# First sublayer's projections as three products of high and low halves, on one core of a Trainium2 chip

## The chip, the cores and the metric

The kernel runs on one core of one Trainium2 chip. The metric is the device time of one execution in microseconds (us), as the median of several executions; lower is better. The engines are named as in the profile: PE (TensorE, matrix products; PEld is its weight load), DVE (VectorE), ACT (ScalarE), POOL (GpSimd), and SP, which here only issues DMAs. Each runs its own list of instructions in order and waits on semaphores that the others raise.

## The reference

Four rows of 1024 tokens with 128 features pass through four sublayers, each behind a layer norm and added to its input: a linear-attention block, a mixture of 32 experts, a windowed attention, and the same mixture again. The change touches the first sublayer. Cut to it:

```python
def _L0_attn_a_ref(x, Wq, Wk, Wv, lambda_params, g1, g2, g3, W1, W2):
    xn = _rms(x, g1)                                   # x is the layer norm of the input
    Q, K, V = xn @ Wq.T, xn @ Wk.T, xn @ Wv.T          # as 16 heads of 8
    pQ, pK = elu(Q), elu(K)
    Q1, Q2 = split(pQ); K1, K2 = split(pK)             # halves of a head
    kv1, kv2 = K1 (x) V * SCALE, K2 (x) V * SCALE      # summed over the heads of a token
    attn = Q1 kv1 - lmb * Q2 kv2
    attn = (1.0 - LAMBDA_INIT) * _rms(attn, g2)
    attn = _rms(attn, g3) + attn
    return gelu(attn @ W1) @ W2 + attn
x = x + _L0_attn_a_ref(_layernorm(x), ...)
x = x + _L0_ffn_ref(_layernorm(x), gate_w, gate_up_w, down_w)      # 32 experts, 8 per token
x = x + _L0_attn_b_ref(_layernorm(x), w_qkv, w_out, b_out)         # window of 64
x = x + _L0_ffn_ref(_layernorm(x), gate_w, gate_up_w, down_w)
```

## The kernel before, in words

A row of 1024 tokens is two groups of 512 (T = 4 tiles of 128 tokens). The mixture of experts is the bulk of the work: each pass of a group through it is a stage of 16 chunks (two experts each). In a chunk PE forms gate and up with six products of 512 columns (high and low halves of inputs and weights, lines 1489 to 1491), ACT applies silu (L1030), DVE multiplies by up (L1270), POOL multiplies by the token's weight for the expert (L847), and three chunks later PE multiplies by `down_w` in plain fp32 (L1512, two instructions per product). Everything else is fitted between chunks as named steps. A table written by hand (`PLAN`, `SPECIAL`) says behind which chunk of which stage each step is done; `AHEAD` does the same for the start, before the first stage. Every engine walks the same table and does its own part of each step, so a step's place in the table is its place in the order of every engine that has a part in it.

The steps of the first sublayer for a group are `x_stats` (DVE), `x_rstd` (POOL), `x_apply` (ACT, writes the normed tiles `z`), `x_turn` (PE transposes `z` into the PSUM bank `side`, ACT copies it to `zT`), then four times `qkv` (PE multiplies a tile of `zT` by `qkv_a_w`, 384 columns; ACT copies it to `qkv` and starts `elu`), `attend` (POOL, `kv_terms`), `kvsum`, `wterm`, `wred` (DVE), the norms per head and token `h_sq1` to `h_gain`, and `h_sum` (DVE), which writes `attn_sum`; `x_add` (POOL) and `attnT` (PE) read that. The projections come under three names: `qkv_first` for the first group of row 0, `qkv_next` for the first group of row 1, `qkv` for the others.

All steps that use the bank `side` take turns. Before PE writes it, it waits until the semaphore `side_taken` has counted every earlier use as taken (`side_free`). A use is taken when its reader has finished; for `x_turn` that is ACT's copy into `zT`:

```python
def copy_side(dst, row, name, n):
    side_product(row, name, n)
    act.activation(dst, side, ACT.Copy).then_inc(side_taken, 1)
```

`x_turn` runs eight times (ACT line 897, output `zT`): at 10, 28, 58, 122, 267, 343, 501 and 572 us of the span. The first three stand in `AHEAD`. In it, DVE's order before the change at the second one is `elu_first` 3, then `kvsum` 1, since `x_turn` has no part on DVE.

Of the kernel before, what the change touches and what calls it, by code (L numbers as in the profile page):

```python
# [80 lines left out]
def back(*steps):  # L81
# [246 lines left out]
AHEAD = own(  # L328
    ("masks", 0), ("x_stats", 0), ("x_rstd", 0), ("x_apply", 0), ("x_stats", 1), ("w_hi", 0), ("masks", 1), ("x_rstd", 1),
    ("x_turn", 0), ("qkv_first", 0), ("qkv_first", 1), ("lam", 0), ("elu_first", 0), ("attend", 0), ("qkv_first", 2),  # L330
    ("elu_first", 1), ("qkv_first", 3), ("kvsum", 0), ("elu_first", 2), ("attend", 1), ("wterm", 0), ("wred", 0),
# [89 lines left out]
def hybrid_block(nc, x, wqkv_a, lam, g1, g2, g3, w1, w2, wqkv_b, wout, bout, wgate, wg, wu, wd, out):  # L421
# [3 lines left out]
    with ExitStack() as ctx:  # L425
        def sb(name, shape, dt=F32):
            return ctx.enter_context(nc.sbuf_tensor(name, shape, dt))

        def sem(name):
            return ctx.enter_context(nc.semaphore(name))  # L430


        qkv_a_w = sb("qkv_a_w", [P, 3 * D])
        w1_w, w2_w = sb("w1_w", [P, D]), sb("w2_w", [P, D])
# [24 lines left out]

        zT = sb("zT", [P, GT])  # L460
        qkv = sb("qkv", [P, T, 3 * D])
        elu = sb("elu", [P, T, 2 * D])
        kv_terms, w_terms = sb("kv_terms", [P, 2, HD * HD * H]), sb("w_terms", [P, H * HD * HD])
        kv = sb("kv", [P, HD * HD])
        attn, squares = sb("attn", [P, G, T, D]), sb("squares", [P, T, D])
        head_ms, head_rms = sb("head_ms", [P, T * H]), sb("head_rms", [P, T * H])
        newton = sb("newton", [P, T * H])
        tok_ms, tok_rms = sb("tok_ms", [P, T]), sb("tok_rms", [P, T])
        gain = sb("gain", [P, T, D])
        attn_sum = sb("attn_sum", [P, T, D])  # L470
        attnT = sb("attnT", [P, GT])
# [21 lines left out]
        mixT = sb("mixT", [P, TILES, P])  # L493
        mix_all = sb("mix_all", [P, NB * P])

        bank = [ctx.enter_context(nc.psum_tensor(f"bank{i}", [P, 512], F32))[:] for i in range(8)]
# [5 lines left out]
        gate_loaded, up_loaded = sem("gate_loaded"), sem("up_loaded")  # L502
        pool_const, ident_ready, masks_ready = sem("pool_const"), sem("ident_ready"), sem("masks_ready")
        lam_step, qkv_w_ready, bits_ready, head_mask_ready = (
            sem("lam_step"), sem("qkv_w_ready"), sem("bits_ready"), sem("head_mask_ready"))
# [37 lines left out]

        qkv_a_loads = [(qkv_a_w[:], wqkv_a), (g1_col[:], g1.rearrange("(p a) -> p a", a=1))]
        attn_a_loads = [(lam_row[:], lam.partition_broadcast(P)), (g2_row[:], g2.partition_broadcast(P)),
# [3 lines left out]
        def wait(engine, semaphore, count):  # L549

            if count > 0:
                engine.wait_ge(semaphore, count)
# [4 lines left out]
        def group(row, g):  # L557
            return row * G + g
# [164 lines left out]
        def _(pool):  # L723
# [105 lines left out]
            def x_add(row, g):  # L829
                pool.wait_ge(attn_ready, group(row, g) + 1)  # L830
                x = x_of(row)[:, T * g:T * g + T]
                pool.tensor_tensor(x, x, attn_sum[:], ALU.add).then_inc(attn_added, 1)

# [53 lines left out]
        def _(act):  # L887
# [22 lines left out]
            def x_turn(row, g):  # L910
                copy_side(zT[:], row, "x_turn", g)

# [178 lines left out]
        def _(dve):  # L1091
# [7 lines left out]
            def norm_stats(row, kind, n):  # L1099
# [104 lines left out]
            def h_sum(row, g):  # L1204
                dve.wait_ge(gain_ready, group(row, g) + 1)
                wait(dve, attn_a_done, group(row, g))
                dve.tensor_tensor(attn_sum[:], attn[:, g], gain[:], ALU.mult).then_inc(attn_ready, 1)

# [57 lines left out]
            def gated(row, f, s):  # L1266
# [6 lines left out]
            steps = {"x_stats": lambda row, n: norm_stats(row, "x", n), "m_stats": lambda row, n: norm_stats(row, "m", n),  # L1273
                     "s_stats": lambda row, n: norm_stats(row, "s", n), "lam": lam_step_coef, "elu": elu_step, "elu_first": elu_of_first, "w_hi": w_hi, "w_lo": w_lo, "kvsum": kvsum, "wterm": wterm, "wred": wred,
                     "h_red1": h_red1, "h_newton1": h_newton1, "h_newton2": h_newton2, "h_scale": h_scale, "h_red2": h_red2, "h_sum": h_sum, "mlp2": mlp2,
# [3 lines left out]
            dve.wait_ge(qkv_a_loaded, 16 * len(qkv_a_loads))  # L1279
            dve.tensor_scalar(qkv_a_w[:], qkv_a_w[:], g1_col[:, 0:1], None, ALU.mult).then_inc(qkv_w_ready, 1)  # L1280
            dve.wait_ge(attn_a_loaded, 16 * len(attn_a_loads))
# [3 lines left out]
            step(dve.tensor_scalar(g2_row[:], g2_row[:], 1.0 - LAMBDA_INIT, None, ALU.mult))  # L1285
            run_ahead(steps, 2)

# [70 lines left out]
        def _(pe):  # L1358
# [3 lines left out]
            def turn(row, kind, n, name):  # L1362
# [4 lines left out]
                mm.then_inc(side_ready, 1)  # L1367

            def qkv_step(row, i):
                side_free(row, "qkv", i)  # L1370
                t = i % T
                pe.matmul(side[:, 0:3 * D], zT[:, P * t:P * (t + 1)], qkv_a_w[:],  # L1372
                          start=True, stop=True).then_inc(side_ready, 1)

            def qkv_first(row, i):
                if i == 0:
                    pe.wait_ge(qkv_w_ready, 1)
                    pe.wait_ge(side_taken, SIDE_AT[0, "x_turn", 0] + 1)
                pe.matmul(bank[i][:, 0:3 * D], zT[:, P * i:P * (i + 1)], qkv_a_w[:],
                          start=True, stop=True).then_inc(qkv_first_ready, 1)  # L1380

            def qkv_next(row, i):
                if i == 0:
                    pe.wait_ge(side_taken, SIDE_AT[row, "x_turn", 0] + 1)
                if i > 1:
                    pe.wait_ge(next_taken, i - 1)
                pe.matmul(bank[NEXT_BANKS[i % 2]][:, 0:3 * D], zT[:, P * i:P * (i + 1)], qkv_a_w[:],
                          start=True, stop=True).then_inc(next_ready, 1)

            def attnT_step(row, g):  # L1390
                pe.wait_ge(attn_ready, group(row, g) + 1)
                side_free(row, "attnT", g)
                for t in range(T):
                    mm = pe.transpose(side[:, P * t:P * (t + 1)], attn_sum[:, t], ident[:])
                mm.then_inc(side_ready, 1)
# [251 lines left out]
```

## Time and profile before

| | |
|---|---|
| median of 3 runs | 1011.01 us (1008.63 to 1011.54) |
| profiled execution, its own time | 1018.66 us |
| its span | 1016.9 us |
| busy: PE, DVE, ACT, POOL | 917.2, 643.8, 612.5, 660.4 us |
| granted PE clock, mean | 0.956 of 2.4 GHz |

The span runs from the first to the last instruction of the profiled execution; its own time is 1.8 us more. PE is busy for 90% of the span. Its first 100 us are different from the rest: there PE has little to do, and the other engines hand one group's work to each other.

### The profile page before, as it was taken

What the parts mean: (1) busy time and instruction counts of PE and PEld (TensorE: products, weight loads), DVE (VectorE), ACT (ScalarE), POOL (GpSimd) and SP (SyncE); (2) the same over time, 40 slices, a digit from 0 to 9 for tenths busy, and PEclk for the clock granted to TensorE, in tenths of its full rate; (3) what the DMA queues carried; (4) which work ended last, traced back from release to release, by engine and by line L of the source; (5) the groups of instructions that cost most, each with busy time, mean ns of one, the idle gap of its engine ahead of it and who ended that gap; (6) DMA issues with size and microseconds to landing.
All of it is one profiled execution on the core that took longest, in us unless ns stands there. A gap on an engine that the chain in (4) does not pass through costs nothing.

```text
span 1016.9 us, 16679 instructions
## 1 busy us (share of the span) xinstructions
PE 917.2 (90%) x5472; PEld 629.8 (62%) x5472; DVE 643.8 (63%) x1447; ACT 612.5 (60%) x1876; POOL 660.4 (65%) x610
## 2 busy tenths in 40 slices
PE   2366999899999999899999899999999998998998
PEld 1144656676666666587666556677666566666665
DVE  4877865687759647688739636778744247447432
ACT  4444756984664576876674566698465458376432
POOL 6676967566778749556759746756665446545654
PEclk8558999999999999979999999999999999999999
DMA  5004361114453544510433544530344661260362
GB/s 181 0 1 97 82 127 44 43 44 101 92 125 85 128 92 90 132 38 17 94 85 86 124 90 89 124 83 17 70 100 86 125 142 39 63 147 13 83 127 62
DMA packets 63320, 85.67 MB, mean 84 GB/s; under 512 B 3777, under 2 KB 29186, under 8 KB 62978
## 3 DMA queue, kind: packets, MB, share of 16 engines
q1 hardware_dynamic: 63234, 84.61, 36.8%
q8 instruction: 43, 0.70, 0.3%
q14 instruction: 43, 0.35, 0.1%
HBM read 79.32 MB, written 5.28 MB: 83 GB/s over the span
## 4 chain that ended last, share of the span: by engine, by line
PE 58%; ACT 14%; POOL 8%; DVE 7%; issue 5%; DMA 1%; DVEq 0%; SPq 0%; ACTq 0%; POOLq 0%
PE bank L1512 16%; PE bank L1489 8%; PE bank L1491 8%; PE bank L1490 8%; ACT probs L1055 6%; PE bank L1533 3%; POOL work L847 3%; PE bank L1548 3%; PE bank L1562 2%; POOL kv_terms L812 2%; ACT work L1030 1%; PE bank L1526 1%; POOL probs L855 1%; PE bank L1372 1%; PE bank L1366 1%
## 5 line engine op out<-in xcount | busy, mean ns | idle before, releaser
L847 POOL TENSOR_TENSOR work<-work,spread_w 128x512 f32<-128x512 f32 x256 | 338.3, 1333 | 179.8 <-DVE work L1270 155.6
L1270 DVE TENSOR_TENSOR work<-work,bank 128x512 f32<-128x512 f32 x256 | 174.4, 682 | 227.9 <-ACT work L1030 143.3
L1512 PE MATMUL bank<-work,down_w 128*128 128x512 f32 x512 | 266.1, 604 | 14.2 <-POOL work L847 9.1
L1030 ACT ACTIVATE work<-bank 128x512 f32<-128x512 f32 x256 | 150.9, 595 | 182.3 <-PE bank L1491 179.3
L1055 ACT ACTIVATE probs<-bank,neg_max 128x96 f32<-128x96 f32 x512 | 166.0, 383 | 12.3 <-DVE neg_max L1298 6.5
L1489 PE MATMUL bank<-z_hi,gate_hi 128*128 128x512 f32 x256 | 169.0, 660 | 2.5 <-ACT work L1030 1.8
L855 POOL TENSOR_TENSOR probs<-probs,prob_inv 128x768 f32<-128x768 f32 x64 | 94.1, 1470 | 73.0 <-DVE prob_inv L1306 73.0
L1055 ACT ACTIVATION_READ_ACCUMULATOR probs<-bank,neg_max 128x1 f32 x512 | 126.8, 250 | 0.0
L1512 PEld LDWEIGHTS bank<-work,down_w 128*128 128x128 f32 x512 | 95.6, 191 | 44.4 <-POOL work L847 14.5
L1491 PE MATMUL bank<-z_hi,gate_lo 128*128 128x512 f32 x256 | 102.1, 399 | 0.0
L1491 PE MATMUL bank<-z_hi,up_lo 128*128 128x512 f32 x256 | 101.8, 398 | 0.0
L1489 PE MATMUL bank<-z_hi,up_hi 128*128 128x512 f32 x256 | 101.8, 398 | 0.0
L1490 PE MATMUL bank<-z_lo,gate_hi 128*128 128x512 f32 x256 | 101.6, 397 | 0.0
L1490 PE MATMUL bank<-z_lo,up_hi 128*128 128x512 f32 x256 | 100.9, 394 | 0.0
L812 POOL TENSOR_TENSOR kv_terms<-elu,qkv 128x1024 f32<-128x1024 f32 x32 | 81.6, 2553 | 17.9 <-DVE elu L1127 14.8
L1312 DVE COPY probsT<-bank 96x512 f32<-96x512 f32 x128 | 80.3, 666 | 5.0 <-PE bank L1548 4.7
L1298 DVE TENSOR_REDUCE neg_max<-bank 128x4 f32<-128x384 f32 x128 | 64.9, 548 | 24.7 <-PE bank L1533 23.7
L1548 PE MATMUL bank<-ident,probs 128*96 128x128 f32 x512 | 71.4, 282 | 10.2 <-DVE probsT L1312 8.4
L1489 PEld LDWEIGHTS bank<-z_hi,gate_hi 128*128 128x128 f32 x256 | 49.1, 192 | 40.2 <-issue 30.5
L1533 PE MATMUL bank<-keysT,qm 32*128 32x96 f32 x1024 | 70.7, 273 | 0.0
L1490 PEld LDWEIGHTS bank<-z_lo,gate_hi 128*128 128x128 f32 x256 | 49.3, 193 | 34.1 <-issue 31.3
L1548 PEld LDWEIGHTS bank<-ident,probs 128*96 128x96 f32 x512 | 54.2, 128 | 23.0 <-issue 13.3
(154 smaller groups left out, 1481.0 us busy)
## 6 DMA issues: line engine op xcount, KB each, us to landing
spread_w<-comb_dram SPq DMA_DIRECT2D x126, 512.0 KB, 6.7
vals<-v_dram SPq DMA_DIRECT2D x16, 384.0 KB, 4.0
x_buf<-x SPq DMA_DIRECT2D x8, 256.0 KB, 3.2
v_dram<-v_tok SPq DMA_DIRECT2D x8, 256.0 KB, 5.0
out<-xs SPq DMA_DIRECT2D x8, 256.0 KB, 4.2
spread_w<-wg SPq DMA_DIRECT2D x1, 1024.0 KB, 7.2
spread_w<-wu SPq DMA_DIRECT2D x1, 1024.0 KB, 9.3
comb_dram<-combT SPq DMA_DIRECT2D x16, 64.0 KB, 1.6
```

Of the source, the lines that this page charges most:

```text
L812: pool.tensor_tensor(kv_terms[:, i % 2].rearrange("p (e d h) -> p e d h", e=HD, d=HD), k.unsqueeze(2).broadcast_to([P, HD, HD, H]), v.unsq ...
L847: pool.tensor_tensor(work[:, n % WORK], work[:, n % WORK], spread_w[:, n // EACH % 2, s % EACH], ALU.mult).then_inc(hid_gated, 1)
L855: pool.tensor_tensor(pr, pr, prob_inv[:, i % 2, part].unsqueeze(2).broadcast_to([P, HALF_BLOCKS, KW]), ALU.mult).then_inc(probs_normed, 1)
L1030: act.activation(work[:, n % WORK], bank[GATE_BANKS[ring_of(row, f, s)]], ACT.Silu).then_inc(silu_ready, 1)
L1055: a = act.activation(probs[:, i % 2, m], bank[hg][:, b * KW:(b + 1) * KW], ACT.Exp, bias=neg_max[:, i % 2, m:m + 1], accum_out=prob_sum[:, ...
L1270: dve.tensor_tensor(work[:, n % WORK], work[:, n % WORK], bank[UP_BANKS[ring_of(row, f, s)]], ALU.mult).then_inc(gated_ready, 1)
L1489: pe.matmul(dst, w_hi[:, cols], h, start=True, stop=False)
L1490: pe.matmul(dst, w_hi[:, cols], l, start=False, stop=False)
L1491: pe.matmul(dst, w_lo[:, cols], h, start=False, stop=True).then_inc(ready, 1)
L1512: pe.matmul(bank[Y_BANK], down_w[:, c], work[:, n % WORK], start=(c == 0), stop=(c == CH - 1)).then_inc(down_done, 1)
L1533: mm = pe.matmul(bank[hg][:, KW * b:KW * (b + 1)], qm[feats, i // T, NB * (i % T) + b].rearrange("p j q -> p (j q)"), keysT[feats, first:f ...
L1548: mm = pe.transpose(bank[4 + b % 2][0:KW, P * hg:P * (hg + 1)], probs[:, i % 2, hg * NB + b], ident[:])
```

## The change

The weights `qkv_a_w` and the turned inputs `zT` are each split into a high half (a copy rounded to F32R) and a low half (what the copy left out). Each projection is then three products instead of one fp32 product. The low half of the input is formed by DVE out of the bank `side`, so `x_turn` gets a part on DVE, `x_lo`; the bank is taken when that has run. The weights are split by DVE in two more instructions at the start. `x_turn` 0 is moved ahead in `AHEAD`. `squares` and `gain` share one buffer, the raw weights are loaded into `mix_all`, and `h_sum` writes its product over `attn`, so `attn_sum` and a wait go.

```diff
 AHEAD = own(
-    ("masks", 0), ("x_stats", 0), ("x_rstd", 0), ("x_apply", 0), ("x_stats", 1), ("w_hi", 0), ("masks", 1), ("x_rstd", 1),
-    ("x_turn", 0), ("qkv_first", 0), ("qkv_first", 1), ("lam", 0), ("elu_first", 0), ("attend", 0), ("qkv_first", 2),
+    ("masks", 0), ("x_stats", 0), ("x_rstd", 0), ("x_apply", 0), ("x_turn", 0), ("x_stats", 1), ("w_hi", 0),
+    ("masks", 1), ("x_rstd", 1), ("qkv_first", 0), ("qkv_first", 1), ("lam", 0), ("elu_first", 0), ("attend", 0), ("qkv_first", 2),
...
-        attn, squares = sb("attn", [P, G, T, D]), sb("squares", [P, T, D])
+        attn, scratch = sb("attn", [P, G, T, D]), sb("scratch", [P, T, D])
+        squares = gain = scratch
...
+        qkv_a_w = mix_all[:, 0:3 * D]
...
             def x_turn(row, g):
-                copy_side(zT[:], row, "x_turn", g)
+                side_product(row, "x_turn", g)
+                act.activation(zT_hi[:], side, ACT.Copy).then_inc(x_hi_ready, 1)
...
+            def x_lo(row, g):
+                dve.wait_ge(x_hi_ready, group(row, g) + 1)
+                dve.tensor_tensor(zT_lo[:], side, zT_hi[:], ALU.subtract).then_inc(side_taken, 1)
...
             def h_sum(row, g):
                 dve.wait_ge(gain_ready, group(row, g) + 1)
-                wait(dve, attn_a_done, group(row, g))
-                dve.tensor_tensor(attn_sum[:], attn[:, g], gain[:], ALU.mult).then_inc(attn_ready, 1)
+                dve.tensor_tensor(attn[:, g], attn[:, g], gain[:], ALU.mult).then_inc(attn_ready, 1)
...
-            dve.tensor_scalar(qkv_a_w[:], qkv_a_w[:], g1_col[:, 0:1], None, ALU.mult).then_inc(qkv_w_ready, 1)
+            step(dve.tensor_scalar(qkv_a_w, qkv_a_w, g1_col[:, 0:1], None, ALU.mult))
+            step(dve.tensor_copy(qkv_a_hi[:], qkv_a_w))
+            dve.tensor_tensor(qkv_a_lo[:], qkv_a_w, qkv_a_hi[:], ALU.subtract).then_inc(qkv_w_ready, 1)
+            x_lo(0, 0)
...
+            def project(dst, t, ready):
+                h, l = zT_hi[:, P * t:P * (t + 1)], zT_lo[:, P * t:P * (t + 1)]
+                pe.matmul(dst, h, qkv_a_hi[:], start=True, stop=False)
+                pe.matmul(dst, h, qkv_a_lo[:], start=False, stop=False)
+                pe.matmul(dst, l, qkv_a_hi[:], start=False, stop=True).then_inc(ready, 1)
+
             def qkv_step(row, i):
                 side_free(row, "qkv", i)
-                t = i % T
-                pe.matmul(side[:, 0:3 * D], zT[:, P * t:P * (t + 1)], qkv_a_w[:],
-                          start=True, stop=True).then_inc(side_ready, 1)
+                project(side[:, 0:3 * D], i % T, side_ready)
```

`qkv_first` and `qkv_next` call `project` in the same way, and `x_add` and `attnT` read `attn[:, g]`.

The order of DVE's instructions changes where `x_lo` enters. At the second `x_turn` of the start, where the sums of the first group's tiles follow each other (`elu` is `elu_first`, `kv` is `kvsum`, `w_terms` is `wterm`, `attn` is `wred`), DVE had before:

```order
16 L1162 TENSOR_TENSOR w_terms<-elu,kv 128x1024
17 L1168 TENSOR_REDUCE attn<-w_terms 128x128
18 L1132 SCALAR_TENSOR_TENSOR elu<-elu,qkv 128x256
19 L1138 TENSOR_REDUCE kv<-kv_terms 128x8x8
20 L1162 TENSOR_TENSOR w_terms<-elu,kv 128x1024
21 L1168 TENSOR_REDUCE attn<-w_terms 128x128
```

and has now, from the same tile on:

```order
19 L1168 TENSOR_TENSOR w_terms<-elu,kv 128x1024
20 L1174 TENSOR_REDUCE attn<-w_terms 128x128
21 L1138 SCALAR_TENSOR_TENSOR elu<-elu,qkv 128x256
22 L1123 TENSOR_TENSOR zT_lo<-bank,zT_hi 128x512
23 L1144 TENSOR_REDUCE kv<-kv_terms 128x8x8
24 L1168 TENSOR_TENSOR w_terms<-elu,kv 128x1024
25 L1174 TENSOR_REDUCE attn<-w_terms 128x128
```

The subtraction stands between the last `elu_first` and `kvsum` 1, and with it DVE's wait for the turned and copied tiles of the second group.

At the `x_turn` of row 3's first group (501 us before), in the slot behind chunk 9 of a stage, DVE had before the choice of experts (`MAX`, `neg_top`, `MATCH_REPLACE`), `h_sum`, and the next chunks' products (`work`):

```order
507 L1241 MAX top<-logits 128x8 x4
508 L1243 TENSOR_SCALAR neg_top<-top 128x4
509 L1245 MATCH_REPLACE replaced<-top,logits 128x32 x4
510 L1207 TENSOR_TENSOR attn_sum<-attn,gain 128x512
511 L1270 TENSOR_TENSOR work<-work,bank 128x512 x2
```

and has now:

```order
515 L1246 MAX top<-logits 128x8 x4
516 L1248 TENSOR_SCALAR neg_top<-top 128x4
517 L1250 MATCH_REPLACE replaced<-top,logits 128x32 x4
518 L1212 TENSOR_TENSOR attn<-attn,scratch 128x512
519 L1123 TENSOR_TENSOR zT_lo<-bank,zT_hi 128x512
520 L1275 TENSOR_TENSOR work<-work,bank 128x512 x2
```

The subtraction, which frees the bank for the first projection of that group behind chunk 10, comes last of the slot's steps.

## Rows read from the trace of the kernel before

**Rows 1.** The page, chain that ended last, shares of the span by engine.

```profile
PE 58%; ACT 14%; POOL 8%; DVE 7%; issue 5%; DMA 1%; DVEq 0%; SPq 0%; ACTq 0%; POOLq 0%
```

**Rows 2.** The chain in order of time, 264 to 270 us: start, us, what.

```profile
267.73 0.23 PE bank L1491
267.96 0.86 PE bank L1512 x2
268.82 0.65 PE bank L1372 x2
```

**Rows 3.** A group of DVE by line and shape: busy us, mean ns, idle before.

```profile
L1225 DVE TENSOR_TENSOR z_lo<-bank,z_hi 128x512 fp32r<-128x512 f32 x16 | 11.0, 685 | 5.1 <-ACT z_hi L981 5.1
```

**Rows 4.** Timeline of the first projections: start, us, engine, line, [idle before, releaser].

```profile
10.59 0.16 DVE L1282 TENSOR_TENSOR lam_prod<-lam_row 128x2 f32<-128x2 f32 x1 [5.30 <-DMA router_w<-wgate]
10.76 5.29 PE L1379 MATMUL bank<-qkv_a_w,zT 128*128 128x384 f32 x8 [0.78 <-ACT zT L897]
...
12.42 0.49 ACT L922 ACTIVATE qkv<-bank 128x384 f32<-128x384 f32 x1 [1.80 <-PE bank L1379]
...
13.70 0.49 ACT L922 ACTIVATE qkv<-bank 128x384 f32<-128x384 f32 x1
```

**Rows 5.** Timeline of DVE, 23 to 37 us.

```profile
23.26 1.30 DVE L1132 SCALAR_TENSOR_TENSOR elu<-elu,qkv 128x256 f32<-128x256 f32 x1
24.48 1.21 DVE L1138 TENSOR_REDUCE kv<-kv_terms 128x64 f32<-128x1024 f32 x1
...
34.48 1.22 DVE L1168 TENSOR_REDUCE attn<-w_terms 128x128 f32<-128x1024 f32 x1
36.48 0.69 DVE L1173 TENSOR_REDUCE head_ms<-squares 128x64 f32<-128x512 f32 x1 [0.77 <-ACT squares L959]
```

**Rows 6.** Timeline of ACT at the second turn.

```profile
24.99 1.63 ACT L906 ACTIVATE z<-x_buf,shift,rstd 128x128 f32<-128x128 f32 x4
27.83 0.60 ACT L897 ACTIVATE zT<-bank 128x512 f32<-128x512 f32 x1 [1.20 <-PE bank L1366]
```

**Rows 7.** Timelines of DVE, PE and ACT at the third turn.

```profile
57.95 1.19 DVE L1138 TENSOR_REDUCE kv<-kv_terms 128x64 f32<-128x1024 f32 x1
...
58.76 2.93 PE L1387 MATMUL bank<-qkv_a_w,zT 128*128 128x384 f32 x4 [0.69 <-ACT zT L897]
...
61.78 0.49 ACT L939 ACTIVATE qkv<-bank 128x384 f32<-128x384 f32 x1 [0.57 <-PE bank L1387]
...
62.44 1.64 ACT L906 ACTIVATE z<-x_buf,shift,rstd 128x128 f32<-128x128 f32 x4
```

**Rows 8.** Timelines of DVE and POOL, on to the first weighted chunk.

```profile
65.91 0.69 DVE L1225 TENSOR_TENSOR z_lo<-bank,z_hi 128x512 fp32r<-128x512 f32 x1 [4.21 <-ACT z_hi L981]
...
88.05 1.27 POOL L847 TENSOR_TENSOR work<-work,spread_w 128x512 f32<-128x512 f32 x1
```

**Rows 9.** Timeline of DVE, end of the choice of experts at 268 us.

```profile
268.61 0.17 DVE L1245 MATCH_REPLACE8 replaced<-top,logits 128x32 f32<-128x32 f32 x1
```

**Rows 10.** The chain and DVE's timeline at row 3's first turn.

```profile
502.92 0.65 PE bank L1372 x2
...
503.43 0.69 DVE L1207 TENSOR_TENSOR attn_sum<-attn,gain 128x512 f32<-128x512 f32 x1
```

**Rows 11.** Timelines of ACT, DVE and PE behind row 3's second turn.

```profile
571.53 0.60 ACT L897 ACTIVATE zT<-bank 128x512 f32<-128x512 f32 x1 [1.23 <-PE bank L1366]
...
571.51 1.28 DVE L1187 TENSOR_SCALAR newton<-head_ms 128x64 int32<-128x64 int32 x1
...
573.83 0.88 DVE L1113 BATCH_NORM_STATS2 stats<-xs 128x6 f32<-128x128 f32 x4
...
580.93 0.63 PE L1366 MATMUL bank<-ident,z 128*128 128x128 f32 x4 [2.26 <-DVEq L1216]
```

**Rows 12.** A long wait of PE, and the stretch behind it (PEclk is the granted clock).

```profile
806.48 1.13 PE L1446 MATMUL bank<-seqT,qkv_b_w 128*128 128x512 f32 x2 [2.02 <-DVEq L1216]
...
808.00:810.00 2.00, 2.00 (x6) 1.52 (x6) 0.00 (x0) 2.00 (x5) 0.00 (x0) 0.50 0.00 0
```

More of the change, by code:

```diff
@@ L430, in sem @@
             return ctx.enter_context(nc.semaphore(name))
-        qkv_a_w = sb("qkv_a_w", [P, 3 * D])
+        qkv_a_hi, qkv_a_lo = sb("qkv_a_hi", [P, 3 * D], F32R), sb("qkv_a_lo", [P, 3 * D], F32R)
         w1_w, w2_w = sb("w1_w", [P, D]), sb("w2_w", [P, D])
@@ L458, in hybrid_block @@
         z = sb("z", [P, NORM_RING, T, D])
-        zT = sb("zT", [P, GT])
+        zT_hi, zT_lo = sb("zT_hi", [P, GT], F32R), sb("zT_lo", [P, GT], F32R)
         qkv = sb("qkv", [P, T, 3 * D])
@@ L468, in hybrid_block @@
         tok_ms, tok_rms = sb("tok_ms", [P, T]), sb("tok_rms", [P, T])
-        gain = sb("gain", [P, T, D])
-        attn_sum = sb("attn_sum", [P, T, D])
         attnT = sb("attnT", [P, GT])
@@ L503, in hybrid_block @@
         pool_const, ident_ready, masks_ready = sem("pool_const"), sem("ident_ready"), sem("masks_ready")
+        x_hi_ready = sem("x_hi_ready")
         lam_step, qkv_w_ready, bits_ready, head_mask_ready = (
@@ L542, in hybrid_block @@
         head_added = sem("head_added")
-        qkv_a_loads = [(qkv_a_w[:], wqkv_a), (g1_col[:], g1.rearrange("(p a) -> p a", a=1))]
+        qkv_a_loads = [(qkv_a_w, wqkv_a), (g1_col[:], g1.rearrange("(p a) -> p a", a=1))]
         attn_a_loads = [(lam_row[:], lam.partition_broadcast(P)), (g2_row[:], g2.partition_broadcast(P)),
@@ L831, in x_add @@
                 x = x_of(row)[:, T * g:T * g + T]
-                pool.tensor_tensor(x, x, attn_sum[:], ALU.add).then_inc(attn_added, 1)
+                pool.tensor_tensor(x, x, attn[:, g], ALU.add).then_inc(attn_added, 1)
             steps = {"w_lo": w_lo, "masks": masks, "attend": attend, "h_rg": h_rg, "h_pow2": h_pow2, "x_add": x_add,
@@ L1273, in _ @@
             steps = {"x_stats": lambda row, n: norm_stats(row, "x", n), "m_stats": lambda row, n: norm_stats(row, "m", n),
-                     "s_stats": lambda row, n: norm_stats(row, "s", n), "lam": lam_step_coef, "elu": elu_step, "elu_first": elu_of_first, "w_hi": w_hi, "w_lo": w_lo, "kvsum": kvsum, "wterm": wterm, "wred": wred,
+                     "s_stats": lambda row, n: norm_stats(row, "s", n), "x_turn": x_lo, "lam": lam_step_coef, "elu": elu_step, "elu_first": elu_of_first, "w_hi": w_hi, "w_lo": w_lo, "kvsum": kvsum, "wterm": wterm, "wred": wred,
                      "h_red1": h_red1, "h_newton1": h_newton1, "h_newton2": h_newton2, "h_scale": h_scale, "h_red2": h_red2, "h_sum": h_sum, "mlp2": mlp2,
@@ L1285, in _ @@
             step(dve.tensor_scalar(g2_row[:], g2_row[:], 1.0 - LAMBDA_INIT, None, ALU.mult))
-            run_ahead(steps, 2)
+            run_ahead(steps, 5)
             dve.wait_ge(bits_ready, 1)
@@ L1378, in qkv_first @@
                     pe.wait_ge(side_taken, SIDE_AT[0, "x_turn", 0] + 1)
-                pe.matmul(bank[i][:, 0:3 * D], zT[:, P * i:P * (i + 1)], qkv_a_w[:],
-                          start=True, stop=True).then_inc(qkv_first_ready, 1)
+                project(bank[i][:, 0:3 * D], i, qkv_first_ready)
             def qkv_next(row, i):
@@ L1386, in qkv_next @@
                     pe.wait_ge(next_taken, i - 1)
-                pe.matmul(bank[NEXT_BANKS[i % 2]][:, 0:3 * D], zT[:, P * i:P * (i + 1)], qkv_a_w[:],
-                          start=True, stop=True).then_inc(next_ready, 1)
+                project(bank[NEXT_BANKS[i % 2]][:, 0:3 * D], i, next_ready)
             def attnT_step(row, g):
@@ L1393, in attnT_step @@
                 for t in range(T):
-                    mm = pe.transpose(side[:, P * t:P * (t + 1)], attn_sum[:, t], ident[:])
+                    mm = pe.transpose(side[:, P * t:P * (t + 1)], attn[:, g, t], ident[:])
                 mm.then_inc(side_ready, 1)
```

## The prediction

> **What bounds the kernel now.** I read the page first, for the chain that ended last: more than half of it is PE [rows 1]. That share is a mean over two different stretches, so I then read the chain in order of time. From about 100 us on PE's products stand in it back to back over long stretches: a product of high and low halves takes a place of 0.23 us at 512 columns, an fp32 product of 512 columns 0.86, and a projection of 384 columns 0.65 [rows 2]. There, what a step costs PE is what it costs the kernel, and 17 of the 20 projections that fall behind 100 us are pieces of that chain. Before 100 us PE hardly counts. I read the timelines of the other engines there and looked for the one whose instructions leave no gap. It is DVE: from the `elu` at 23.26 to the `wred` that starts at 34.48 each instruction starts as the one before it ends, and ACT's squares and the norms follow on that last sum [rows 5]. The chain goes on with `z_lo` at 65.91 and ends at POOL's first weighted chunk at 88.05 [rows 8]; in between, each engine waits for the one before it, and nothing there is tied to a fixed time such as a load from outside.
>
> **Splitting the weights** adds two DVE instructions of 384 columns in a stretch where DVE sits idle for 5.30 us [rows 4]. A subtraction of 512 columns takes 0.685 us [rows 3], so both together stay under 1.4 us. They cost nothing; without that cover they would cost about that.
>
> **The first turn.** The bank was free for PE when ACT's copy ended, and PE began at 10.76 [rows 4]. Now DVE's subtraction follows the copy. Nearest row: `z_lo`, the same instruction, 0.685 us [rows 3]. So PE begins at about 11.40. The products themselves get shorter. A projection here takes 1.28 us (ACT's copies of the first two start 12.42 and 13.70), twice the 0.65 of rows 2: PE is at 1.2 GHz, not 2.4. Three products of 384 columns are 3 x 0.23 x 384/512 = 0.52 us at full clock, so 1.04 here. ACT's first copy came 1.66 us after PE's start, which is one projection and 0.38 of tail; now 11.40 + 1.04 + 0.38 = 12.82, later by **0.4 us**. ACT's three instructions per tile take as long as the projection did, so the delay stays.
>
> **The second turn** is the main term. DVE now has the subtraction between `elu` and `kvsum` 1, and it waits there for a row of hand-overs that DVE did not wait for before: ACT norms the second group from 24.99, PE turns it, and ACT's copy starts at 27.83 and ends at 28.43 [rows 6]. None of this can start earlier, since ACT does it after its part for the tile whose `elu` DVE has just finished. The subtraction ends at 28.43 + 0.04 + 0.69 = 29.1 or so. Queued behind it are nine sums of DVE that started at 24.48 [rows 5]; POOL waits for `kvsum` 1 before its fourth `attend`, ACT waits for the last `wred`. All of that is later by 29.1 - 24.5 = **4.6 us**. Bounds: 0.69 if the wait were covered, 4.7 if nothing is; DVE's rows leave no gap until 35.7, so I take the upper one. The gaps that DVE has later (0.77 before the head sums, 4.21 before `z_lo`) are waits for ACT and PE working on that same late group, and do not absorb it.
>
> **The third turn.** ACT's copy ended by 58.7; `kvsum` runs to 59.14 and stands ahead of the subtraction [rows 7]. So the bank is free at 59.9 and not at 58.76. The second projection is ready at 59.9 + 2 x 1.04 + 0.38 = 62.4 where ACT took it at 61.78, and ACT's `m_apply` (62.44) stands behind it: **0.6 us** on the way to `z_lo`. The start is later by 0.4 + 4.6 + 0.6 = 5.6 us.
>
> **The products behind 100 us.** 0.65 - 0.52 = 0.13 us less each, 17 times in the chain: **-2.2 us**. Bounds: nothing, if three weight loads instead of two show, and 20 x 0.16 = -3.2 if every projection counts and three quarters of its time is left. The Trainium skill, "FP8 and Floating Point Precision", section TensorE Precision Notes, says that true fp32 takes four passes through the array. By that, three passes in place of four leave 0.49 us, a little more gain than my rows give; the trace's 0.86 to 0.23 us is nearly that four.
>
> **The five later turns.** Here PE turns the tiles behind one chunk and wants the bank back behind the next one, a good two microseconds later. Whether DVE is through by then I read at each turn.
> - 267 us: the choice of experts stands ahead of the subtraction and ends at 268.78 [rows 9]. With 0.69 the bank is free at 269.5. PE came for it at 268.82 [rows 2]: it waits **0.7 us**.
> - 501 us: ahead of the subtraction stands `h_sum` too, from 503.43 [rows 10]. It gives way at 504.04 or so, the subtraction ends at 504.7. PE came at 502.92: it waits **1.9 us**. Queued behind it on PE are all products of the next chunk, which need nothing from DVE.
> - 572 us: no step stands ahead, but DVE waits for ACT's copy, which ends at 572.13 [rows 11], and is through at 572.85. Before, it was in the small instructions of the head norms from 571.5 on [rows 11]. The next thing is the statistics at 573.83, on which m_rstd, `m_apply` and PE's turn at 580.93 depend, and PE already waits 2.26 us there. Of the 1.5 us about 1.0 is made good, for one of those small instructions took 1.28 us while POOL was at work beside it, and would now come after that: **0.5 us**.
> - 122 and 343 us: read in the same way, the subtraction is through just as PE arrives, or before. Nothing.
>
> Together **+3.1 us**. Bounds: 0 and 5.
>
> **The shared buffers and `h_sum` in place.** The steps that write and read `scratch` already follow one another through semaphores, and the wait that goes was one for work long done. Same instructions, same sizes: nothing, either way.
>
> **The sum** is 5.6 - 2.2 + 3.1 = +6.5 us, on the profiled execution's own 1018.66 us: 1025.1, 0.64% more. The median of the runs shown is 0.75% lower than that execution; the same share on 1011.01 gives **1017.4 us**.
>
> **Rivals.**
> - *The waits of PE also cost clock.* After a wait of 2.02 us the granted clock was 0.50 for the next microseconds [rows 12]; a chunk at that clock takes about twice its 6 x 0.23 + 0.86 = 2.2 us. The wait that I forecast at 501 us is nearly as long, and the one at 580.93 gets longer. One such stretch of a chunk is 2.1 us: 1019.5. Against it: at 501 us PE has been dense before. Chance 0.2.
> - *The start absorbs most of the 4.6.* If POOL or ACT, not DVE, set the pace from 24 to 48 us, the delay of DVE would fill its gaps; 0.7 of it is left, the sum is 2.6 less 0.5: some 2 us, 1013. Chance 0.16. Against it: the closed row of DVE instructions.
> - *Faster: DVE's part is covered everywhere and the shorter products count everywhere.* The place where it decides is the start. If ACT's waits for a product (its copies at 12.42 and later) are what paces it, eight projections at the low clock save 8 x 0.24 = 1.9 us there, with 20 x 0.13 = 2.6 later: 4.5 us less, 1006.5. It decides once the subtraction at 28.4 us delays no `kvsum`. For it speaks that ACT does wait for each projection in the start; against it, that DVE's `kvsum` 1 did not wait for any of these. Chance 0.07.
> - *Worse than summed:* the late group shifts chunks, POOL's and DVE's work meets otherwise, and another turn than I read makes PE wait: up to 1023. Chance 0.07.
>
> My forecast itself has 0.5, with a range of its own of 1015 to 1019. A difference under 0.3% can't be told from none here. 1014.0 is that bound: the likeliest case, the clock and the worse case lie above it (0.77); the absorbed start within it (0.16); the rest is faster. The range is 1012 to 1022.
>
> **What would show it.** In the profile after: DVE idle for some 4 us before `zT_lo` near 25 us, and the first `kvsum` behind it at about 29.5; POOL's first weighted chunk at about 93.6 where it was at 88.05; projections of 0.52 us in the chain; PE waiting for `zT_lo` before a projection for about 0.7 and 1.9 us at the fifth and the seventh turn, near 273 and 508. It is wrong if the first weighted chunk comes less than 4 us later, or if the projections' saving is 0.2 us and more.

## The result, and the profile after

| | before | changed |
|---|---|---|
| median, us | 1009.97 (4 runs, 1008.63 to 1011.54) | 1021.83 (4 runs, 1018.78 to 1025.7) |
| ratio | | 1.0108, 95% interval 1.0072 to 1.0144 |
| the profiled execution: its own time, its span, us | 1018.66, 1016.9 | 1020.7, 1018.9 |

The changed kernel is slower by 7.3 to 14.5 us. The two profiled spans are only 2.0 us apart, because the profiled execution of before ran at half clock for some 10 us where no other profile here does (last section). So below the profiles are compared at the same instruction, and from the start on.

The first turn, a timeline of the changed kernel (columns as in [rows 4]):

```profile
10.89 0.69 DVE L1123 TENSOR_TENSOR zT_lo<-bank,zT_hi 128x512 fp32r<-128x512 f32 x1 [4.48 <-ACT zT_hi L913]
11.73 0.66 PE L1379 MATMUL bank<-qkv_a_hi,zT_hi 128*128 128x384 f32 x1 [1.50 <-DVE zT_lo L1123]
...
13.06 0.49 ACT L924 ACTIVATE qkv<-bank 128x384 f32<-128x384 f32 x1 [2.21 <-PE bank L1381]
```

ACT takes the first projection at 13.06, 0.64 later than in [rows 4]. DVE at the second turn:

```profile
23.72 1.30 DVE L1138 SCALAR_TENSOR_TENSOR elu<-elu,qkv 128x256 f32<-128x256 f32 x1
28.92 0.69 DVE L1123 TENSOR_TENSOR zT_lo<-bank,zT_hi 128x512 fp32r<-128x512 f32 x1 [3.90 <-ACT zT_hi L913]
29.53 1.21 DVE L1144 TENSOR_REDUCE kv<-kv_terms 128x64 f32<-128x1024 f32 x1
...
41.45 0.69 DVE L1179 TENSOR_REDUCE head_ms<-scratch 128x64 f32<-128x512 f32 x1 [0.70 <-ACT scratch L961]
```

`elu` comes 0.46 later than in [rows 5], `kv` 5.05 later: the turn itself costs 4.59. DVE stands idle for 3.90 us behind `elu`, and the last sum and the norms behind it are as late (`head_ms` 4.97). The third turn, DVE's and ACT's timelines:

```profile
62.91 1.19 DVE L1144 TENSOR_REDUCE kv<-kv_terms 128x64 f32<-128x1024 f32 x1
64.02 0.68 DVE L1123 TENSOR_TENSOR zT_lo<-bank,zT_hi 128x512 fp32r<-128x512 f32 x1
...
65.86 1.22 DVE L1174 TENSOR_REDUCE attn<-w_terms 128x128 f32<-128x1024 f32 x1
...
67.16 0.49 ACT L941 ACTIVATE qkv<-bank 128x384 f32<-128x384 f32 x1 [0.28 <-PE bank L1381]
...
70.66 0.60 ACT L983 ACTIVATE z_hi<-bank 128x512 fp32r<-128x512 f32 x1 [1.20 <-PE bank L1374]
```

`kv` is now 4.96 later than in [rows 7], ACT's second copy of a projection 5.38. And POOL's first weighted chunk:

```profile
93.14 1.26 POOL L848 TENSOR_TENSOR work<-work,spread_w 128x512 f32<-128x512 f32 x1
```

It was at 88.05 [rows 8]: 5.1 later. The later turns, PE's waits by releaser (us in total, times, longest) and its timelines at the fifth and the seventh:

```profile
PE bank L1379 <- DVE zT_lo L1123: 7.4, 5, 1.8
```

```profile
274.25 0.44 PE L1379 MATMUL bank<-qkv_a_hi,zT_hi 128*128 128x384 f32 x1 [0.94 <-DVE zT_lo L1123]
274.54 0.34 PE L1380 MATMUL bank<-qkv_a_lo,zT_hi 128*128 128x384 f32 x1
...
505.15 0.44 PE L1379 MATMUL bank<-qkv_a_hi,zT_hi 128*128 128x384 f32 x1 [1.84 <-DVE zT_lo L1123]
505.43 0.34 PE L1380 MATMUL bank<-qkv_a_lo,zT_hi 128*128 128x384 f32 x1
...
509.85 1.02 PE L1522 MATMUL bank<-work,down_w 128*128 128x512 f32 x2
...
510.89 0.34 PE L1380 MATMUL bank<-qkv_a_lo,zT_hi 128*128 128x384 f32 x1
511.07 0.34 PE L1381 MATMUL bank<-qkv_a_hi,zT_lo 128*128 128x384 f32 x1
511.24 0.39 PE L1499 MATMUL bank<-z_hi,gate_hi 128*128 128x512 f32 x1
```

A projection in the flow of PE: the down products take 0.86 from 509.85, and the next chunk starts at 511.24, so its place is 0.53 us, 0.12 less than in [rows 2]. After a wait the second product comes 0.28 us behind the first and not 0.17: a wait costs a little more than its idle time. The eighth turn, DVE's timeline:

```profile
574.22 0.69 DVE L1123 TENSOR_TENSOR zT_lo<-bank,zT_hi 128x512 fp32r<-128x512 f32 x1 [0.79 <-ACT zT_hi L913]
574.82 0.18 DVE L1192 TENSOR_SCALAR head_ms<-head_ms 128x64 f32<-128x64 f32 x1
575.04 0.20 DVE L1193 TENSOR_SCALAR newton<-head_ms 128x64 int32<-128x64 int32 x1
...
576.28 0.87 DVE L1115 BATCH_NORM_STATS2 stats<-xs 128x6 f32<-128x128 f32 x4
```

The small instruction of 1.28 us in [rows 11] takes 0.20 here, as forecast.

### The profile page after: what moved, and what is told of

Read it like the earlier page. It is cut to its first block, busy times and chain, and to the rows that moved or that the text cites. A ratio compares the mean times of both kernels' runs of the same rounds, so it can differ in the third digit from the quotient of the medians.

```text
span 1018.9 us, 16751 instructions
## 1 busy us (share of the span) xinstructions
PE 907.9 (89%) x5504; PEld 632.5 (62%) x5504; DVE 646.8 (63%) x1457; ACT 612.7 (60%) x1876; POOL 660.4 (65%) x610
## 4 chain that ended last, share of the span: by engine, by line
PE 56%; ACT 13%; DVE 8%; POOL 8%; issue 5%; DMA 2%; SPq 0%; DVEq 0%; ACTq 0%; POOLq 0%
PE bank L1522 16%; PE bank L1499 8%; PE bank L1501 8%; PE bank L1500 7%; ACT probs L1057 6%; PE bank L1543 3%; POOL work L848 3%; PE bank L1558 3%; PE bank L1572 2%; DMA spread_w<-comb_dram 1%; PE bank L1536 1%; DVE work L1275 1%; DVE probsT L1320 1%; POOL kv_terms L813 1%; PE bank L1374 1%
## 5 line engine op out<-in xcount | busy, mean ns | idle before, releaser
L1499 PE MATMUL bank<-z_hi,gate_hi 128*128 128x512 f32 x256 | 163.0, 637 | 3.5 <-ACT elu L942 2.2
```

The source lines that it names most:

```text
L1499: pe.matmul(dst, w_hi[:, cols], h, start=True, stop=False)
```

## The experiments

Each kernel was timed beside the kernel before. Eleven were run, in five groups. The table has in each row one instruction of ACT and how much later (+) it starts in the profile of a kernel than in that of the kernel before with only its buffers shared (`buffers_alone`). That one is the reference because its profile lacks the 10 us at half clock. The choice matters: against it the profile of before itself stands at +1.20 by 257 us, +6.22 at 618 and +7.37 at the end. A load that POOL waits for at 136 us lands 1.0 us later in it; most of the rest is those 10 us.

| at, us | `after` | `changed_again` | `start_and_turns` | `eighth_alone` | `high_first` | `products_alone` | `two_products` |
|---|---|---|---|---|---|---|---|
| z_hi, 65.24 | +5.42 | +5.59 | +1.72 | +1.78 | +1.83 | -0.21 | -0.41 |
| z_hi, 257.35 | +5.69 | +2.60 | +2.29 | +0.57 | +0.67 | -0.01 | -1.70 |
| combT, 276.76 | +6.55 | +3.45 | +1.95 | +0.22 | +0.33 | -0.35 | -2.59 |
| z_hi, 487.22 | +6.21 | +3.51 | +1.98 | +2.84 | +0.24 | -0.15 | -3.93 |
| combT, 505.78 | +8.34 | +7.22 | +1.98 | +2.87 | +0.25 | -0.39 | -4.53 |
| v_tok, 618.28 | +8.09 | +5.39 | +1.76 | +2.20 | -0.45 | -1.09 | -6.29 |
| yT, 1004.7 | +9.33 | +6.54 | +2.88 | +3.62 | +1.21 | +0.05 | -0.57 |

Stretches of some 4 us at half clock move these columns too; one costs 1.1 to 1.6 us against a profile without it. The reference has them at 154, 240 and 574 us, and none from 700 to 815, where the others have one: that makes most of the step between the last two rows. `eighth_alone` and `high_first` have the second at 222 us in place of 240. They lose 0.7 us to the reference by 235 us and gain 1.8 from there to 245. A window of `buffers_alone`, then the same of `high_first` (the granted clock, PEclk, is the third number from the right):

```profile
242.00:244.00 2.00, 2.00 (x30) 1.51 (x23) 0.79 (x2) 0.00 (x0) 0.00 (x0) 0.60 1.06 203
...
242.00:244.00 2.00, 2.00 (x41) 1.74 (x40) 0.69 (x1) 0.00 (x0) 0.00 (x0) 1.00 1.09 227
```

**The waits, moved one by one.** `start_later` moves DVE's part of the second turn behind the next sums; `turns_early` puts it first in slot 9 at the fifth and the seventh turn (the diff shows one of the two slots); `start_and_turns` does both.

```diff
-    ... ("wterm", 1), ("wred", 1), ("qkv", 4),
+    ... ("wterm", 1), ("wred", 1), ("x_low", 1), ("qkv", 4),
...
-        9: back(("top", 2)) + own(("h_sum", 1), ("x_add", 1)) + ahead(("x_turn", 0)),
+        9: ahead(("x_low", 0)) + back(("top", 2)) + own(("h_sum", 1), ("x_add", 1)) + ahead(("x_turn", 0)),
```

> The changed kernel, but DVE's subtraction of the second turn stands behind wred 1 and not ahead of kvsum 1 in the start. My theory (DVE's wait there, 3.9 us of idle and 0.6 of work, moves the whole start): kvsum 1 goes back to about 24.9 us, only the 0.6 us of work stays, the first weighted chunk of POOL comes about 4 us sooner than in the changed kernel, and the time is about 4 us less (1.007 of before where the changed kernel was 1.011). Rival (the start absorbs the wait, the loss lies elsewhere): the same as the changed kernel within 1 us.

> The changed kernel, but at the fifth and the seventh turn DVE's subtraction stands ahead of the choice of experts and of h_sum. My theory (PE waits 0.9 and 1.8 us for the bank there): both waits go, the time is 2 to 3 us less than the changed kernel's (1.008 of before). Rival (the waits are made good later): no change within 1 us.

> Both moves together. My theory: what is left is 0.5 us at the first turn, 0.6 at the second, 0.6 at the third, 0.6 at the eighth, less 2 us of shorter products, so 0 to 1 us over before (1.000 to 1.001). If the ratio stays at 1.004 or more, there is a cost of 4 us that neither the start nor the two waits of PE hold, and that the pair of profiles does not show.

Measured: 1.0060 (1.0036 to 1.0084), 1.0049 (1.0032 to 1.0066) and 1.0020 (0.9997 to 1.0042), at 1018.37, 1016.44 and 1013.6 us where before had 1011.84. In `start_later` DVE's idle time at the second turn is 0.20 us:

```profile
27.50 1.22 DVE L1174 TENSOR_REDUCE attn<-w_terms 128x128 f32<-128x1024 f32 x1
28.91 0.69 DVE L1123 TENSOR_TENSOR zT_lo<-bank,zT_hi 128x512 fp32r<-128x512 f32 x1 [0.20 <-ACT zT_hi L913]
```

Its first `z_hi` stands at +1.74, not at +5.42. With both moved, most of the slowdown is gone: PE no longer waits for `zT_lo` at the fifth and the seventh turn (three waits of 4.6 us in all are left, those of the start). `turns_early` came out better than the 1.008 expected. In its profile it is 4.5 us ahead of the changed kernel at 618 us: 3.0 behind 257 us, where the two turns are, and 1.5 ahead of it, where its half-clock stretch lies at 226 us and not at 240.

**The waits without the shorter products, the products without the waits, the buffers without either.** In `waits_alone` each projection is one fp32 product of the high halves, with DVE's part kept (both low halves are left out of the result). In `products_alone` the third product reads the high half again and DVE has no part (the low half of the inputs is left out). `buffers_alone` is the kernel before with the shared scratch, the raw weights in `mix_all` and `h_sum` in place. `changed_again` is the changed kernel, unchanged.

```diff
 waits_alone
+                pe.matmul(dst, h.bitcast(F32), qkv_a_hi[:].bitcast(F32), start=True, stop=True).then_inc(ready, 1)
 products_alone
-                act.activation(zT_hi[:], side, ACT.Copy).then_inc(x_hi_ready, 1)
+                act.activation(zT_hi[:], side, ACT.Copy).then_inc(side_taken, 1)
-                pe.matmul(dst, l, qkv_a_hi[:], start=False, stop=True).then_inc(ready, 1)
+                pe.matmul(dst, h, qkv_a_hi[:], start=False, stop=True).then_inc(ready, 1)
```

> The turns and their subtraction as in the changed kernel, but each projection is one fp32 product of the high halves as before (the output lacks both low halves). My theory: the start's wait and PE's waits without the shorter products, so 2 to 3 us more than the changed kernel, 9 us over before (1.009 to 1.012). Rival (the products themselves are the loss): faster than the changed kernel.

> Three products per projection, but no low half of the inputs: the third product reads the high half again, the bank is freed by ACT's copy as before, and DVE has no part in the turns (the output lacks the low half's share). My theory: the start as before or up to 1 us sooner, 17 projections in the chain 0.13 us shorter: 2 to 3.5 us faster than before (0.997 to 0.998). Rival (three weight loads instead of two show, or the products cost clock): no faster than before, or slower.

> The kernel before with only the shared buffers, h_sum in place and the raw weights in mix_all. Both theories: 1.000, within 1 us of before; each step at its place of before within 0.1 us. If shared buffers do add a wait, the norms of a group come later in the profile.

> The changed kernel once more, with many executions of it and of before side by side. My theory: the aligned profiles show a shift of 6.6 us at the end once a stretch of half clock that only the profiled execution of before had is taken out; so the ratio settles at 1.0065 to 1.009. Rival (a further cost of 4 us that shows in the times and not in the pair of profiles): 1.011 again.

Measured: `waits_alone` 1.0115 (1.0091 to 1.0138), `products_alone` 0.9991 (0.9974 to 1.0009), `buffers_alone` 0.9993 (0.9978 to 1.0009), `changed_again` 1.0090 (1.0065 to 1.0115). The waits carry the whole slowdown, the buffers nothing that can be measured, and the products less than a measurement tells. The interval of `changed_again` holds what I expected and the rival's 1.011 too. Its profile also has what stands in the prediction as a rival, a fall of the clock behind a wait of PE. Its timeline and windows behind the seventh turn:

```profile
502.46 0.44 PE L1379 MATMUL bank<-qkv_a_hi,zT_hi 128*128 128x384 f32 x1 [1.86 <-DVE zT_lo L1123]
...
503.19 0.63 PE L1499 MATMUL bank<-z_hi,gate_hi 128*128 128x512 f32 x1
503.62 0.63 PE L1500 MATMUL bank<-z_lo,gate_hi 128*128 128x512 f32 x1
```

```profile
502.00:504.00 2.00, 1.54 (x5) 1.39 (x6) 1.00 (x2) 0.57 (x2) 2.00 (x2) 0.74 0.82 154
504.00:506.00 2.00, 2.00 (x6) 1.56 (x5) 0.00 (x0) 1.97 (x3) 0.40 (x1) 0.50 0.00 0
506.00:508.00 2.00, 2.00 (x9) 1.22 (x9) 1.36 (x4) 0.55 (x2) 1.10 (x1) 0.91 0.00 0
```

and the windows of the first profile of the changed kernel at the same turn:

```profile
504.00:506.00 2.00, 0.85 (x4) 0.82 (x5) 1.69 (x3) 0.69 (x5) 1.43 (x2) 1.00 1.07 213
506.00:508.00 2.00, 2.00 (x8) 1.27 (x7) 0.00 (x0) 1.98 (x3) 1.11 (x1) 1.00 0.21 38
```

The same kernel and nearly the same wait (1.86 and 1.84): one execution falls to 1.2 GHz at its end and the other stays at 2.4. From 487 to 506 us in the table the first loses 3.7 us and the second 2.1: the clock's part is 1.6 us. Of the four profiles with this wait (`after`, `changed_again`, `start_later`, `waits_alone`) it is the only one. That the wait set it off is not shown, since such stretches also come where PE did not wait (last section).

**All turns placed.** `all_placed` also puts the subtraction ahead of `kvsum` 5 at the third turn, and behind `m_stats` at the eighth; `eighth_alone` only the latter, on top of `start_and_turns`.

```diff
-    ("x_apply", 0)) + own(("m_stats", 0), ("m_rstd", 0), ("kvsum", 5)) + ahead(
+    ("x_apply", 0)) + own(("m_stats", 0), ("m_rstd", 0)) + ahead(("x_low", 0)) + own(("kvsum", 5)) + ahead(
...
-        3: ahead(("x_turn", 1), ("h_newton1", 0)) + back(("m_stats", 3), ("m_rstd", 3)),
+        3: ahead(("x_turn", 1), ("h_newton1", 0)) + back(("m_stats", 3), ("m_rstd", 3)) + ahead(("x_low", 1)),
```

> Both moves of the subtraction, and two more: at the third turn ahead of kvsum 5, at the eighth behind the statistics. My theory: 0.5 us less at each than with the first two moves, so level with before or up to 1 us faster (0.998 to 1.001). Rival: no different from the two moves.

> The kernel with DVE's part placed at the second, fifth and seventh turn (1013.6 us, ratio 1.002), and also at the eighth, behind the statistics; the third turn stays as in the changed kernel. The run in which the third and the eighth were both placed came out at 1.005. My theory of that run: the loss of 2.7 us came at the third turn (the sum of the fifth tile late, then stretched beside POOL), and the placement at the eighth gained about 0.5 us. Expected here: ratio 1.0015, z_hi of the first stage at the time of the kernel with two placed turns within 0.1 us, and about 0.5 us gained behind 572 us. Rival, the loss comes from the eighth place or from something else in the later stages: ratio 1.004 or more again.

Measured: 1.0050 (1.0028 to 1.0071), and 0.9998 (0.9977 to 1.0019), medians of 1012.28 and 1011.89 us: level. The first was a miss, in the direction of slower. DVE, POOL and ACT at the third turn of `all_placed`, in three pieces of its timeline:

```profile
60.08 0.69 DVE L1123 TENSOR_TENSOR zT_lo<-bank,zT_hi 128x512 fp32r<-128x512 f32 x1 [0.72 <-ACT zT_hi L913]
60.69 1.21 DVE L1144 TENSOR_REDUCE kv<-kv_terms 128x64 f32<-128x1024 f32 x1
61.99 2.82 DVE L1168 TENSOR_TENSOR w_terms<-elu,kv 128x1024 f32<-128x1024 f32 x1
64.85 1.22 DVE L1174 TENSOR_REDUCE attn<-w_terms 128x128 f32<-128x1024 f32 x1
...
61.36 5.64 POOL L813 TENSOR_TENSOR kv_terms<-elu,qkv 128x1024 f32<-128x1024 f32 x2
...
66.15 0.49 ACT L941 ACTIVATE qkv<-bank 128x384 f32<-128x384 f32 x1 [3.19 <-issue]
```

`w_terms` now starts while POOL's product is running and takes 2.82 us in place of 1.22. The sum behind it ends at 66.07, and ACT copies the second projection right then, since it waits for that sum before it overwrites `qkv`. The first `z_hi` stands at +4.40, 2.7 later than in `start_and_turns`. `eighth_alone`, without that move, is back at +1.78, so the third turn was the loss.

**High halves first.** `high_first` is `eighth_alone`, and lets PE begin at the first and the third turn with the two products of the high half; only the third product waits for DVE.

```diff
+                if low:
+                    pe.wait_ge(side_taken, low)
                 pe.matmul(dst, l, qkv_a_hi[:], start=False, stop=True).then_inc(ready, 1)
...
-                    pe.wait_ge(side_taken, SIDE_AT[0, "x_turn", 0] + 1)
-                project(bank[i][:, 0:3 * D], i, qkv_first_ready)
+                    pe.wait_ge(x_hi_ready, 1)
+                project(bank[i][:, 0:3 * D], i, qkv_first_ready, SIDE_AT[0, "x_turn", 0] + 1 if i == 0 else 0)
```

> The same as the one before, and at the first and the third turn PE begins the two products of the inputs' high half once ACT's copy is there, and only the third product waits for DVE's low half (these projections write banks of their own, so nothing forbids that). My theory: the 0.4 us of the first turn and the 0.4 of the third are then hidden behind those two products: the first copy by ACT of a projection comes at about 12.5 instead of 13.06 us, the first stage begins about 0.7 us earlier, ratio 1.0008. Rival, DVE's part is late for other reasons, or the later engines absorb it: no difference from the run before, 1.0015.

Measured: 1.0024 (1.0 to 1.0049). The interval holds both 1.0008 and 1.0015, so the profile has to decide, and it shows no gain. PE did start earlier (ACT's first copy at 12.69, though everything ahead of the first turn stands 0.28 later in this profile than in `eighth_alone`), but the first stage did not (+1.83 and +1.78). POOL's timeline says why:

```profile
13.86 1.00 POOL L797 TENSOR_SCALAR var_eps<-moments 128x4 f32<-128x4 f32 x1 [3.50 <-DVE moments L1118]
...
16.41 0.23 POOL L802 TENSOR_SCALAR shift<-mean_rstd 128x4 f32<-128x4 f32 x1
16.61 2.33 POOL L813 TENSOR_TENSOR kv_terms<-elu,qkv 128x1024 f32<-128x1024 f32 x1
```

`kv_terms`, the start of the chain of sums, follows POOL's own norm of the second group without a gap, and that waits for DVE's `moments`, which stand behind the subtraction in DVE's order. At the third turn ACT copied the second projection at 63.58, as in `eighth_alone` (63.53), though PE had made it 0.6 us earlier: the copy waits for the sum that ends at 63.5, and that sum is late because the subtraction stands ahead of it on DVE.

**Two products.** `two_products` is `products_alone` with the third product left out as well (the low half of the inputs and a third of each projection are missing).

```diff
-                pe.matmul(dst, h, qkv_a_lo[:], start=False, stop=False)
-                pe.matmul(dst, h, qkv_a_hi[:], start=False, stop=True).then_inc(ready, 1)
+                pe.matmul(dst, h, qkv_a_lo[:], start=False, stop=True).then_inc(ready, 1)
```

> The kernel with the products alone (no low half of the inputs, no part on DVE; 1011.98 us, ratio 0.9991), with the third product of each projection left out as well, so the low half of the inputs and a third of each projection are missing from the result. It asks whether PE's time in a projection is the kernel's time behind 100 us. If it is (the step of my sum that gave -2.2): 17 x 0.17 = 2.9 us less behind 100 us and about 8 x 0.17 or 8 x 0.34 of little effect in the start, so the ratio goes to 0.9963. Rival, what PE saves is given back at the next hand-over with DVE, ACT or POOL: ratio 0.998 to 0.999, and the profile shows longer waits of PE in place of the products.

Measured: 0.9942 (0.9924 to 0.9961). The place of a projection is 0.34 us now (the down products start at 506.85 and take 0.86):

```profile
506.85 1.02 PE L1520 MATMUL bank<-work,down_w 128*128 128x512 f32 x2
...
507.88 0.34 PE L1379 MATMUL bank<-qkv_a_lo,zT_hi 128*128 128x384 f32 x1
508.05 0.39 PE L1497 MATMUL bank<-z_hi,gate_hi 128*128 128x512 f32 x1
```

That is 0.31 under the fp32 product, times 17 some 5.3 us or 0.9948, inside the interval. What I expected, 0.9963, was counted from the measured median of `products_alone` and lies just outside. In the profile the column falls by 1.1 to 1.2 us across the four projections of each of the last four turns, 4.7 in all (5.0 would be 16 times 0.31). At 122 us nothing is left of the gain by 153 us (-0.20), and 1.5 more come from the half-clock stretch at 240 us that this profile lacks. So PE's time in the projections is the kernel's time at the last four turns, as the sum had it.

## Why the prediction came out as it did

I forecast 1017.4 us, slower by 0.64%; measured were 1.08% and, the second time, 0.90%. The direction, the place and the mechanism were right, the size 2.6 to 4.5 us too small. The 1021.83 us lie above the forecast's own 1015 to 1019 and only just inside the whole range. Point by point, against the terms of the sum:

- **Splitting the weights: nothing.** Right. DVE stands idle for 4.48 us behind it (the row at 10.89).
- **The first turn: 0.4, measured 0.46 at `elu`.** The size came out by luck, for the path was another. ACT's first copy is 0.64 later and not 0.4. But `elu` hangs on POOL's first `kv_terms` (16.40 for 15.93), and that now follows POOL's norm of the second group, which waits for DVE's `moments` behind the subtraction. By `high_first` a faster projection there brings nothing. The 1.2 GHz of this stretch I read from the time of the products; the granted clock in the profile says 1.00 there (last section).
- **The second turn: 4.6, measured 4.59.** Right, and so was the step "DVE's rows leave no gap, so I take the upper bound". The rival of an absorbing start is dead.
- **The third turn: 0.6, measured about 0.4** (5.42 less 5.05 at the `kv` of the second turn). The named path, "The second projection is ready at" 62.4, is wrong: ACT's copy waits for DVE's sum, as `high_first` and `all_placed` showed. I had read what `kvsum` stands ahead of, and not what ACT waits for beside PE.
- **The start together: 5.6, measured 5.4.**
- **The products behind 100 us: -2.2, measured 0.9 to 1.0.** The size of one is right (0.12 to 0.13), and so is what four of them give: in `products_alone` the shift falls by 0.50, 0.53, 0.46 and 0.49 us across the projections of the fifth to the eighth turn, 2.0 in all. What the sum lacks lies between the fifth and the sixth: from 332 to 354 us 0.8 is given back. POOL's weighting there waits for its load from `comb_dram`, and PE for POOL. POOL and PE in `buffers_alone`, then in `products_alone`:

```profile
330.63 1.29 POOL L847 TENSOR_TENSOR work<-work,spread_w 128x512 f32<-128x512 f32 x1 [2.10 <-DMA spread_w<-comb_dram]
332.58 1.10 PE L1511 MATMUL bank<-work,down_w 128*128 128x512 f32 x2 [1.04 <-ACT yT L1047]
...
331.27 1.27 POOL L848 TENSOR_TENSOR work<-work,spread_w 128x512 f32<-128x512 f32 x1 [3.20 <-DMA spread_w<-comb_dram]
332.59 1.13 PE L1521 MATMUL bank<-work,down_w 128*128 128x512 f32 x2 [1.50 <-POOL work L848]
```

  PE has been 0.46 ahead, and stands level at 332.6. This wait of POOL is 2.8 to 4.0 us in all nine profiles with three products and 1.7 to 2.3 in the other four; why, no run shows. I had taken PE's rows for the chain and not asked what is tied to a load. `after` keeps about 1.0 of the term (8.09 less 5.4, 1.2, 2.1 and 0.4 for the waits). The clock is not the reason in these two: up to 618 us their half-clock stretches are those of the reference. `high_first` goes from +1.83 to -0.45 by 618 us, 2.3 like the sum, but that is luck: 1.2 of it comes before 257 us, where `products_alone` gains nothing (-0.21 to -0.01) and this profile has its half-clock stretch elsewhere, and 1.1 behind, as in `products_alone`. By the Trainium skill, "FP8 and Floating Point Precision", section TensorE Precision Notes, true fp32 takes four passes. An estimate from that, three passes for four, would leave 0.49 us; the trace has 0.53, so it agrees nearly.
- **The fifth turn: 0.7, measured 1.2; the seventh: 1.9, measured 2.1.** The steps are the right ones, mis-sized: PE's idle rows are 0.94 and 1.84, and the first product after a wait takes 0.1 us more. At the fifth DVE was through 0.2 us later relative to PE than I worked out from before. Measured here are the steps in the table around each (5.69 to 6.55 and 6.21 to 8.34), each compared with `start_and_turns` over the same rows.
- **The eighth turn: 0.5, measured about 0.4** (the step from 563 to 596 us is +0.06 in `after` and -0.33 in `eighth_alone`). In the latter the stretched instruction of 1.29 us is back, which bears out the argument that it would pass.
- **The shared buffers: nothing.** Right, 0.9993.
- **The waits cost clock (rival, 0.2).** One profile of four with the wait has such a fall, worth 1.6 us where the rival said 2.1. It may be part of what my median lacked; how many of the timed executions had it is not on record.

By its profile the changed kernel is 8.1 us behind at 618 us, where the sum gives 6.5; the medians give 9 to 12. Of the gap of 2.5 to 5.5 us, the turns hold 0.7, the products' missing gain 1.2 (less 0.3 that the start and the eighth turn cost under their terms), and the clock behind the wait at the seventh turn up to 1.6. The rest is not settled: it is smaller than the scatter between executions (1017.48 to 1023.61 for one kernel).

No version came out faster than before with the full computation; the best, `eighth_alone`, is level (0.9998). In it DVE's part still costs 1.8 us in the start, and of the shorter products about 1 us arrives; the difference is below what the times tell.

## What to carry to other kernels

A step that gets a part on another engine puts a wait into that engine's order. Look for what is queued there behind it, and move the new part to where its input is already there, rather than leave it where the step stands. A saving on the busiest engine can be given back where another engine is tied to a load. When a transfer of a bank is made later, read every wait of the instruction that takes it: here a projection was ready 0.6 us earlier and nobody took it. A move that fills one gap can start a DVE instruction just behind a POOL one and lose more than the gap.

## What the runs showed of the hardware

**Half-clock stretches come and go between executions of one kernel.** The windows of the profiled execution of before:

```profile
432.00:438.00 6.00, 5.97 (x59) 4.91 (x61) 3.34 (x8) 5.25 (x32) 2.94 (x2) 0.51 0.01 3
438.00:444.00 6.00, 6.00 (x61) 5.37 (x63) 4.53 (x9) 1.86 (x12) 2.62 (x3) 0.63 0.01 1
```

PE ran at 1.2 GHz for some 10 us of an attention stage in which it was nearly always busy; `buffers_alone` has no such stretch there, and the same instructions stand 4.4 us later in before from there on. `two_products` has one of the kind at 656 to 674 us (granted clock 0.75, 0.50 and 0.90 over windows of 6 us), and gives back 4.6 us there; `eighth_alone` one at 472 to 476. What sets them off no run here shows. Shorter ones, of 4 us, sit at 154 to 160 and 240 to 244 us in most profiles; `changed_again` has neither, and gains 3.0 us by that between 65 and 257 us. In `two_products` the second is missing, and in `high_first`, `eighth_alone` and `turns_early` it lies at 222 to 232. From 178 to 257 us `two_products` gains 1.4 us on the reference by that and the others 1.0, so a difference of that size between two profiles says nothing of the kernels until the stretches are compared. The Trainium skill, "TensorE: Matmul & The Clock Gate", Part 1, says of one kernel's start that the number of its slow products differs between runs; here the same holds in the middle of a kernel, for much longer stretches.

**The granted clock in the profile can miss a half-clock stretch.** At the third turn of the changed kernel the products of 384 columns follow each other after 0.32 us, in the flow at 511 us after 0.17, and yet PEclk says 1.00:

```profile
65.55 0.52 PE L1381 MATMUL bank<-qkv_a_hi,zT_lo 128*128 128x384 f32 x1
65.87 0.52 PE L1379 MATMUL bank<-qkv_a_hi,zT_hi 128*128 128x384 f32 x1
...
64.00:66.00 2.00, 1.25 (x4) 1.25 (x5) 1.97 (x4) 0.00 (x0) 1.83 (x4) 1.00 0.00 0
```

In `changed_again` the same stretch says 0.50, and its first `z_hi` stands within 0.2 us of this one. So the mean clocks of whole executions are no measure here either.

**Of a DVE and a POOL instruction side by side, the one that started later can take more than twice its time.** In `all_placed` `w_terms` starts at 61.99, 0.63 us into POOL's `kv_terms`, and takes 2.82 us in place of 1.22; it ends 1.1 us after that `kv_terms`. At 21.40 in the same profile it starts 0.15 us ahead of `kv_terms`: it takes 1.21, and `kv_terms` takes 3.24 in place of 2.34. The integer step of 0.20 us in the head norms took 1.28 or 1.29 when it started 0.06 us behind POOL's product.
